# A graph-attention kernel whose relation planes are cleared between the first loads, with the adjacency rows of its front in another order

## The reference, cut to what matters

```python
h = relu(layernorm(x))
# layer 0: 8 heads
q = (h[sub] @ Wq.T + bq); k = (h[obj] @ Wk.T + bk)          # sub, obj = rel_pair_index
att = (q * k).sum(-1) / sqrt(64)
scores = zeros(8, n, n).at[:, sub, obj].set(att)
scores = where(adj == 0, -inf, scores);  scores[:, i, i] = 1e-7
x = x + (softmax(scores, axis=2).mean over heads) @ h
# layer 1: 16 heads, dense adjacency mask
h = relu(layernorm(x)); seq = h @ W_seq
...
return x + elu(hidden @ W_out + b_out)
```

## Time and profile before

| | us |
|---|---|
| median of 3 runs | 1186.28 |
| range of the runs | 1185.34 to 1186.77 |
| the profiled execution, its own time | 1189.33 |
| span of the profiled execution, first to last instruction | 1187.4 |
| PE busy | 1102.9 (93%) |
| DVE busy | 952.3 (80%) |
| ACT busy | 806.8 (68%) |
| POOL busy | 122.2 (10%) |

### The profile page before, as it was taken

How to read it: one execution, slowest core, us unless ns; L and a number is a source line. 1 busy time by engine, 2 the same in 40 slices (tenths; PEclk the granted TensorE clock), 3 DMA queues, 4 the chain that set the end, 5 groups by cost and what they waited for, 6 DMA issues and landing times.

```text
span 1187.4 us, 24638 instructions
## 1 busy us (share of the span) xinstructions
PE 1102.9 (93%) x10565; PEld 764.9 (64%) x10565; DVE 952.3 (80%) x1325; ACT 806.8 (68%) x843; POOL 122.2 (10%) x141
## 2 busy tenths in 40 slices
PE   4999969999999999999897899999999999999997
PEld 3444424444444444444343899999999999999843
DVE  3543517988998999998853899999999999999565
ACT  1343326766667766666624999998999999999122
POOL 2678640000000000000000000000000000000011
PEclk9999987999999999999999999999999999999999
DMA  9531544122222121100342111011001111111311
GB/s 343 130 28 16 129 79 100 34 43 64 65 65 54 38 49 46 36 36 27 125 168 101 64 38 38 38 38 38 38 38 38 38 38 38 38 38 38 108 71 71
DMA packets 37245, 77.69 MB, mean 65 GB/s; under 512 B 5653, under 2 KB 13714, under 8 KB 35090
## 3 DMA queue, kind: packets, MB, share of 16 engines
q1 hardware_dynamic: 30402, 65.26, 15.7%
q0 software_dynamic: 6736, 10.86, 6.4%
HBM read 65.39 MB, written 23.21 MB: 75 GB/s over the span
## 4 chain that ended last, share of the span: by engine, by line
PE 75%; DMA 7%; issue 5%; POOL 5%; ACT 5%; DVE 2%; SPq 0%; DVEq 0%; POOLq 0%; ACTq 0%
PE psum L1573 14%; PE psum L737 12%; PE psum L652 11%; PE psum L1570 8%; PE psum L1571 8%; PE psum L1574 8%; DMA rel_planes<-f_ones,f_flat 5%; PE psum L756 5%; PE psum L1668 5%; POOL rel_planes L156 5%; PE psum L707 2%; ACT area_b L947 2%; ACT area_h L1417 2%; DMA rel_planes<-f_h 1%; PE psum L727 1%
## 5 line engine op out<-in xcount | busy, mean ns | idle before, releaser
L1417 ACT ACTIVATE area_h<-area_a,keep 128x2048 fp8e4<-128x2048 f32 x208 | 397.1, 1993 | 1.2 <-DMA area_a<-s_rows 1.2
L1573 PE MATMUL psum<-s_V,area_h 128*128 128x198 bf16 x2048 | 285.5, 248 | 0.0
L1574 PE MATMUL psum<-s_V,late 128*128 128x99 bf16 x2048 | 279.5, 208 | 0.0
L1570 PE MATMUL psum<-s_V,area_h 128*128 128x99 bf16 x2048 | 206.0, 210 | 11.4 <-DVE area_b L1472 10.7
L1571 PE MATMUL psum<-s_V,area_b 128*128 128x99 bf16 x2048 | 205.9, 209 | 0.0
L1573 PEld LDWEIGHTS psum<-s_V,area_h 128*128 128x128 fp8e4 x2048 | 199.4, 97 | 0.1
L1574 PEld LDWEIGHTS psum<-s_V,late 128*128 128x128 fp8e4 x2048 | 199.3, 97 | 0.0
L1570 PEld LDWEIGHTS psum<-s_V,area_h 128*128 128x128 fp8e4 x2048 | 189.5, 98 | 12.8 <-issue 10.9
L1571 PEld LDWEIGHTS psum<-s_V,area_b 128*128 128x128 fp8e4 x2048 | 189.6, 98 | 0.0
L737 PE MATMUL psum<-area_h,f_region 128*128 128x512 f32 x384 | 181.6, 598 | 0.0
L1156 DVE CUSTOM_DVE_ANT_0 area_b<-psum,late 128x1500 f32<-128x1500 f32 x96 | 161.4, 1717 | 24.0 <-PE psum L652 21.6
(11 more groups left out here) (172 smaller groups left out, 1178.0 us busy)
## 6 DMA issues: line engine op xcount, KB each, us to landing
area_a<-s_rows SPq DMA_DIRECT2D x16, 1024.0 KB, 4.8
late<-rel_planes SPq DMA_DIRECT2D x36, 192.0 KB, 2.7
rel_planes<-f_h SPq DMA_DIRECT2D x2, 2304.0 KB, 22.8
area_h<-in_x SPq DMA_DIRECT2D x4, 1024.0 KB, 12.4
keep<-in_adj POOLq DMA_DIRECT2D x16, 256.0 KB, 5.9
f_region<-in_x SPq DMA_DIRECT2D x16, 256.0 KB, 2.7
x<-f_region SPq DMA_DIRECT2D x16, 256.0 KB, 2.0
area_a<-adj_chunks SPq DMA_DIRECT2D x4, 1024.0 KB, 9.0
```

The source lines that it names most:

```text
L1417: act.activation(masks[:, j, :], s1b[:, b, :], ACT.Relu, bias=t["s2"][:, n, 0, j:j + 1], scale=BIG, saturate=False).then_inc(signs, 1)
L1570: pe.matmul(out[:, :, 0:DZ], masks[:, j, cols], V[:, b, j, :, 0:DZ], **first)
L1573: pe.matmul(out, masks[:, j, cols], V[:, b, j, :, :], **first)
L1574: last = pe.matmul(out[:, :, DZ:CZ], nadjT[:, NEAR_TILES.index(j), cols], V[:, b, j, :, DZ:CZ], **then)
```

## The change

Four edits go together. (1) All three planes are cleared from SyncE's queue: plane 0 before x's first part, plane 1 before Wk, plane 2 before Wq; GpSimd clears none. (2) PLANE gives plane 0 to the first two scatters (it was three), then planes 1, 2, 0 in turn; rows 5 and 6 are loaded before scatters 60 and 74. (3) Gather(1) turns rows 2 and 3 (were 2 and 5), gather(2) row 5 alone (were 3 and 6), and row 6 is turned among the scores of tile 0; chunk places and SyncE's stores follow that order. (4) Heads 2 to 7 of tile 0 are scored in pairs (`score`) instead of one by one (`score_head`), with the row's four turns between; on ScalarE relu(0) comes behind row 3's copies, and exps, copies, count and make_low are interleaved.

```diff
-PLANE = (0,) * 3 + tuple((i + 1) % PLANES for i in range(EC - 3))
-LATE_LOADS = {56: ADJ_RING, 72: ADJ_RING + 1}
+PLANE = (0,) + tuple(i % PLANES for i in range(EC - 1))
+LATE_LOADS = {60: ADJ_RING, 74: ADJ_RING + 1}
@@ stage 1, sync
+        sp.wait_ge(zero_set, 1)
+        f.clear_plane(sp, t, 0)
         load_x(0)
+        f.clear_plane(sp, t, 1)
         load_w(K, "L0_gnn_Wk")
-        sp.wait_ge(zero_set, 2)
-        for i in range(1, PLANES):
-            f.clear_plane(sp, t, i)
+        f.clear_plane(sp, t, 2)
         load_w(Q, "L0_gnn_Wq")
@@ stage 1, gpsimd
         pool.wait_ge(zero_set, 2)
-        f.clear_plane(pool, t, 0)
@@ bank_rounds
-    order = adj(1, NU) + adj(2) + adj(NU + 1) + [("h", 0)] + adj(3, NU + 2) + [("proj", 0), ("one", -1), ("h", 1)]
+    order = adj(1, NU) + adj(2, 3) + [("h", 0)] + adj(NU + 1) + [("proj", 0), ("one", -1), ("h", 1)] + adj(NU + 2)
@@ stage 2
-    PLACE = {0: 0, 1: 1, 2: 0, 3: 1, NU: 2, NU + 1: 2, NU + 2: 2}
-    ORDER = (0, 1, NU, 2, NU + 1, 3) + tuple(range(NU + 2, NT))
+    PLACE = {0: 0, 1: 1, 2: 0, 3: 2, NU: 2, NU + 1: 1, NU + 2: 2}
+    ORDER = (0, 1, NU, 2, 3) + tuple(range(NU + 1, NT))
@@ sync
             store_chunk(2)
-            store_chunk(NU + 1)
             load_x(3)
+            store_chunk(3)
             store_x(1)
             for i in range(PLANES):
                 sp.wait_ge(f.related[i], 16 * PLANE.count(i))
             load_related(0)
             load_related(1)
-            store_chunk(3)
-            store_chunk(NU + 2)
+            store_chunk(NU + 1)
             store_x(2)
             load_x(4)
             load_related(2)
+            store_seq(0)
+            store_chunk(NU + 2)
             load_related(3)
-            store_seq(0)
@@ tensor, front
                 for i in range(8):
                     gather(1, i)
-                    turn_adj(2 if i < 4 else NU + 1, i % 4)
+                    turn_adj(3 if i % 2 else 2, i // 2)
                 turn_h(0)
                 score(0, 0)
                 for i in range(8):
                     gather(2, i)
-                    turn_adj(NU + 2 if i % 2 else 3, i // 2)
+                    if i % 2:
+                        turn_adj(NU + 1, i // 2)
                 project(0)
+                score(0, 1)
                 turn_one_and_scores(-1)
                 turn_h(1)
-                for hd in range(2, HA):
-                    score_head(0, hd)
+                turn_adj(NU + 2, 0)
+                score(0, 2)
+                turn_adj(NU + 2, 1)
+                score(0, 3)
+                for q in (2, 3):
+                    turn_adj(NU + 2, q)
@@ scalar, front
                 for q in range(4):
                     copy_adj(2, q)
+                    copy_adj(3, q)
                 for i in range(PLANES):
                     act.wait_ge(f.plane_zero[i], 16)
                 relu(0)
+                copy_h(0)
                 for q in range(4):
                     copy_adj(NU + 1, q)
-                copy_h(0)
-                for q in range(4):
-                    copy_adj(3, q)
-                    copy_adj(NU + 2, q)
+                relu(1)
+                exp(0, 0)
                 projected(0)
+                exp(0, 1)
                 copy_one_and_scores(-1)
-                relu(1)
                 copy_h(1)
-                for hd in range(2):
-                    exp(0, hd)
                 count(0)
-                for hd in range(2, HA):
-                    exp(0, hd)
-                    if hd == 5:
-                        f.make_low(act, 1)
+                exp(0, 2)
+                copy_adj(NU + 2, 0)
+                exp(0, 3)
+                copy_adj(NU + 2, 1)
+                exp(0, 4)
+                exp(0, 5)
+                copy_adj(NU + 2, 2)
+                f.make_low(act, 1)
+                copy_adj(NU + 2, 3)
+                exp(0, 6)
+                exp(0, 7)
                 edges(0)
```

## The result

| | before | after |
|---|---|---|
| median, us | 1186.28 | 1191.04 |
| range of 7 runs each, us | 1185.34 to 1187.15 | 1187.09 to 1193.85 |
| ratio to before, 95% interval | | 1.0041 [1.0024, 1.0058] |
| profiled execution / its span | 1189.33 / 1187.4 | 1193.51 / 1191.6 |

The change costs 4.8 us. The forecast was 1184.3 with a range to 1190.0 and the likeliest sign "faster", so both the sign and the range are wrong.

A forecast was written before the change was run, and what follows sets the result against it. It took TensorE as busy for 93% of the span, with the relation planes setting tile 0's masks: 170.1 + 26.2 + 0.1 = 196.4 against 198.4, 2.0 us earlier, off the median: 1184.3 us, range 1179.5 to 1190.0.

The forecast's parts named there:

- Bound and place: Front up to tile 0's masks: only this part changes; the 989.0 us after tile 1's scores begin stay the same.
- the sum: Front's step estimates: mask (0,0) at 170.1, plus 26.2 and 0.1, puts tile 1's scores at 196.4, 2.0 us earlier.
- The first loads: SyncE's first transfers: TensorE starts 5.9 us later (bounds 4.5 and 6.6), scatter 0 at 10.5 instead of 18.3.
- The scatters: GpSimd's scatters: scatter 9 leads by 4.5 us, the end by 5.5; mask (0,0) at 170.1 (bounds 168 and 173.5).
- Rival C: Scatters: SyncE's burst gives the 4.5 us back; mask (0,0) at 174.5, 2.4 us later, 1188.7; chance 0.10.
- Tile 0's scores: Mask (0,0) to tile 1's scores: 26.2 us instead of 22.8, between 21.9 at full and 29.7 at half clock.
- Rival B: Tile 0's scores: pairs at half clock throughout, 29.7 us with planes at 172.5, 3.9 us later, 1190.2; chance 0.17.
- ScalarE's tail: ScalarE's edges of tile 0, with row 6's copies among the exps: end near 199.7, so no later than before.
- The clock: TensorE in tile 0's scores: partly busy work also lowers the clock; first pair +2.6 us, other two +1.7.
- The range: Whole kernel's time: 1179.5 to 1190.0, leaving out about one in ten on each side.

The follow-up runs named there:

- a1: Changed kernel with the clears and PLANE of before, row loads still before scatters 60 and 74: 1191.48 us, ratio 1.0037.
- f2: Changed kernel with row loads before scatters 66 and 78, row 6's third quarter and make_low ahead of exp 4, and single heads: 1185.12 us, ratio 0.9994.
- a4: Changed kernel with row 5 loaded before scatter 66 and row 6 before scatter 79: 1187.92 us, ratio 1.0013.
- b5: Kernel before with all planes cleared from SyncE's queue and the new PLANE, nothing else: 1186.22 us, ratio 1.0000.
- a9: Changed kernel loading only the first 128 of 512 rows of W_seq, so a smaller first burst: 1189.06 us, ratio 1.0026.
- a8: Changed kernel with row 6's third quarter turned before the last score pair and make_low ahead of exp 4: 1190.29 us, ratio 1.0040.
- b3: Kernel before with heads 2 to 7 of tile 0 scored in pairs, nothing else: 1192.10 us, ratio 1.0043.
- f1: Changed kernel, pairs kept, row loads before scatters 66 and 78, row 6's third quarter and make_low ahead of exp 4: 1187.89 us, ratio 1.0013.
- a2: Changed kernel with heads 2 to 7 of tile 0 scored one by one again: 1190.56 us, ratio 1.0030.
- d1: Changed kernel with single heads, and row 6's third quarter and make_low ahead of exp 4: 1188.57 us, ratio 1.0007.
- e1: Kernel before with the new clears and PLANE, and rows 5 and 6 loaded before scatters 54 and 66: 1187.71 us, ratio 1.0005.
- e2: e1 with VectorE's finish of the third unrelated tile ahead of the join and short filling matmuls around the single heads: 1183.54 us, ratio 0.9981.
- d3: Kernel before with adjacency rows 0 to 3 loaded by one transfer behind scatter 9: 1193.43 us, ratio 1.0054.

## Why the prediction was wrong, point by point

- **Bound and place: right in the main.** What follows tile 1's scores took 988.9 against 989.0 us, though it varies by 7 us over all profiles. Of the two ways to tile 0's scores the text priced that of the planes; in the kernel before TensorE reached head 2 at 178.95, 1.6 us behind the end of mask (0,0), by way of row 6. The 8.8 us wait for row 6 went, h(0)'s turn waited 2.11 us (1.4 above before's 0.69, as said), the late first matmul was covered (a1) as long as the planes were late (f2), and gather(2) ended at 168.1, later than the 165.4 of the sum, but still ahead of the join at 173.22.
- **The first loads: too small.** First matmul 23.35, outside the bounds (19.3 to 21.4): +8.5 us, not 5.9. The step took 6.90 MB ahead of Wk; by 23.35 us the engines had moved 23.35 x 322 = 7.5 MB. At the rate of the earlier trace rows 6.9 MB is 21.4 us, and the text took 20.7; the rest is the 0.6 MB more. What the sum left out is that transfers issued behind share the engines with those ahead: plane 2's clear was issued at 13.31, behind the 8.03 us of Wk's issue, and Wk landed at 23.35. In the same way 257 x 10.0 = 2.6 MB had moved by 10.0 us, more than the 2.44 that plane 0 was to need, and it was not complete. Scatter 0 at 12.58, not 10.5 (bounds 9 and 12); scatter 3 at 29.53, not 26.9; scatter 9 at 40.19, not 38.5. The lead there was 2.8 us, not 4.5.
- **The scatters: the step that failed.** The sum let the lead grow from 4.5 to 5.5 us on the way, with no row for it and although it gave 1 us back to stalls, and held that "putting the row loads behind scatters 60 and 74 costs nothing". SyncE's bursts moved by the start's delay to 124.4 and 150.3, and the row loads at 125.86 and 153.63 fell on them. The stalls grew from 7.8 to 11.0 us and the lead of 2.8 became a lag of 1.8; 1.6 us of that lead had gone before the bursts. Mask (0,0) was at 176.72 instead of 170.1, outside its bounds (168 to 173.5): 6.6 us, more than the whole gain. The text priced a row's load by when it is needed, and not by what its bytes do to the scatters beside it. Moving the row loads gave back 3.1 us (a4) and ended the scatters 6.0 us earlier; b5, whose row loads go out ahead of the bursts, has its last scatter at 159.7, as forecast. How much the planes' lateness costs in the median stays open: the six kernels with these row loads have mask (0,0) at 174.4 us on the mean, 4.3 later than forecast and not 6.6, and a4's gain may have come by the clock. Rival C had this mechanism, with a tenth of the chance.
- **Tile 0's scores: right in this execution, in part by luck.** 26.0 us against 26.2; the pairs took 5.37, 2.79 and 4.08, the first at half clock and the third in part, much as the sum had it (+2.6 and +1.7 us). Other profiles with the pairs in place have 23.5 (a9), 23.6 (a4) and 24.7 (a8), and in all three the first pair ran at full clock. The step was priced against the 22.8 of before. b3 confirms the direction, not the size: 5.7 us for pairs alone against the 3.4 of the sum (26.2 - 22.8), and 2.8 in the changed kernel (f1 against f2). Rival B, the slower side, was right in its sign, not in its 29.7. Against the forecast it was the planes that decided (6.6 us); against the kernel before it was the scores (3.2 of 4.2).
- **ScalarE's tail: sized right, priced wrongly.** The forecast had the edges end at 199.7, 5.1 us behind the last mask (196.4 - 1.8 = 194.6); they ended 4.8 us behind it, at 205.7. The step called that harmless because it was no later than the 200.28 of before. But the masks were to be 2 us earlier too, and a tail of 4.8 us in place of 3.7 takes that back: mask (0,7) to (1,0) took 11.98 us instead of 10.91, 13.4 with faster masks (a2). The medians give it 0.7 us with pairs (a8) and 2.0 with singles (d1 against a2), neither clear of the noise.
- **The clock.** The reading that the clock falls also on partly busy work held: 0.50 over pairs that kept TensorE 5.36 of 5.40 us busy, and 0.79 on the mean over single heads in e1; with filling matmuls e2 had 0.92. Where the Trainium skill (TensorE: Matmul & The Clock Gate, Part 1: The HAM clock gate) says that idleness throttles and activity releases, the trace agrees for the waits of 7.43 us (after) and 3.46 us (b3) ahead of the slow pairs, and for e2, where short waits were filled. It does not bear it out as the only rule: in a8 the third pair took 5.37 us at 0.50 behind 4.6 us (184.0 to 188.6) in which TensorE was busy for 2.01, with no wait above 1.61 us.
- **The range** reached to 1190.0. Its rival C already had late planes and slow pairs at once, 174.5 and 26.2, and came to 1188.7. It took the scatters' whole gain as lost, but not that they could come later than before: with 176.7 and 26.0 the same sum gives 1190.6, and the median was 1191.04. The bound of the planes was set at 173.5, below its own rival's 174.5.

**What stays open.** Why b5 shows nothing in its median although its profiled execution has mask (0,0) at 170.1 was not settled: the last scatter starts between 159.5 and 169.0 us over all the kernels' profiles, what follows tile 1's scores takes 985 to 992 us, and one profile of each is no mean. What makes that last part longer or shorter, with the same instructions, was not looked into. Whether a4 gained by earlier planes or by a shorter wait ahead of the first pair is open too. How large the pure effect of the half clock is, with masks and order fixed, was not isolated: fills came with the early finish.

## What to carry to other kernels

An edit that delays one queue moves every later burst of that queue: before placing other transfers, list what each will meet at its new time, and charge for what it does to the small transfers beside it (here 6.1 us to landing instead of 2.7), not only for when its own data are needed. Pairs that made TensorE and VectorE wait for each other in turn came with waits and with a granted clock of 0.50 behind them, and a few matmuls that compute nothing, shorter than the wait, came with a gain of 4 us (one VectorE step moved beside them). A chain whose shares do not add up to the whole span has broken off: look where it starts before reading what has left it. When undoing the suspected edit gives back less than it cost elsewhere (0.5 against 5.7 us), look for a second engine that was late behind it, and undo both. And where the same instructions take 985 to 992 us from one profile to the next, compare several profiles of one arrangement before pricing a few us from one.

## What the runs showed of the hardware

- One issue on SyncE's queue took 8.03 us (Wk, at 5.24, in the changed kernel) with two clears of 2.36 MB ahead of it.
- A row's load of 256 KB, with a cast, landed 8.7 us after its issue beside a burst, and scatters in the same stretch after a median of 6.1 us, against 2.7 from 85 to 110 us with nothing beside them (changed kernel); a scatter behind a load of 1 MB waited 8.1 us (d3).
- The granted clock was 0.50 over a pair that kept TensorE busy for 5.15 of 5.20 us, with waits of 3.5 us ahead of it and of the pair before (b3), and 1.00 in 3.60 us with 2.87 busy (changed kernel). The same 12 matmuls of a pair took 2.79 us at 1.00 and 5.37 at 0.50.
- Execution time goes together with the mean granted clock, with a correlation of -0.83 to -0.90 among 22 to 30 runs of the kernel before: 0.001 of the clock is 0.65 to 0.8 us of 1186.
